# A product that nothing reads behind each quad's factors in the first edge pass of a graph network kernel

## What is computed

```python
# layer 0: attention over edges (8 heads of 12)
score = exp(clip((K[src] * Q[dst] / sqrt(12) * (edge_attr @ We + be)).sum(-1), -5, 5))
h = segment_sum(V[src] * score, dst) / (segment_sum(score, dst) + 1e-6)
# layer 1: mean and maximum of the neighbours, two batch norms
h_mean = segment_sum(x[src], dst) / deg;  h_max = segment_max(relu(x @ W_pool + b_pool)[src], dst)
# layer 2: sum of x[src] * out_deg[src]**-0.5, times in_deg**-0.5, then a 96x96 product
# layer 3: segment_sum((x @ W)[src] * edge_weight, dst)
```

## Time and profile before

| | |
|---|---|
| median of three runs | 5378.2 us |
| profiled execution, whole | 5363.67 us |
| its span, first to last instruction | 5361.9 us |
| TensorE busy with products | 2806.4 us (52%) |
| GpSimd busy | 3210.7 us (60%) |
| VectorE busy | 1951.3 us (36%) |
| ScalarE busy | 1385.4 us (26%) |
| mean granted TensorE clock | 0.641 of full speed |

### The profile page before, as it was taken

How to read it: one execution, slowest core, us unless ns; L and a number is a source line. 1 busy time by engine, 2 the same in 40 slices (tenths; PEclk the granted TensorE clock), 3 DMA queues, 4 the chain that set the end, 5 groups by cost and what they waited for, 6 DMA issues and landing times.

```text
span 5361.9 us, 59693 instructions
## 1 busy us (share of the span) xinstructions
PE 2806.4 (52%) x16706; PEld 2541.5 (47%) x16706; DVE 1951.3 (36%) x4524; ACT 1385.4 (26%) x4351; POOL 3210.7 (60%) x3366
## 2 busy tenths in 40 slices
PE   5655666665567777777775453333334333333334
PEld 5555666665556666666663332323224222222224
DVE  4544444444456555555556111111113221111224
ACT  2111111111243333333334331111112121111113
POOL 4555555555526666666665666666665666666665
PEclk6666666666658888888887555555556555555556
DMA  6655555555532222223321111111111111111111
GB/s 189 172 149 146 146 150 142 151 149 144 151 103 83 82 83 82 82 83 83 83 79 41 34 35 35 35 34 35 35 34 47 35 34 36 35 35 35 35 35 45
DMA packets 337348, 431.81 MB, mean 81 GB/s; under 512 B 99312, under 2 KB 248675, under 8 KB 336941
## 3 DMA queue, kind: packets, MB, share of 16 engines
q0 software_dynamic: 133120, 245.58, 17.5%
q1 hardware_dynamic: 203917, 182.42, 12.1%
HBM read 406.71 MB, written 21.00 MB: 80 GB/s over the span
## 4 chain that ended last, share of the span: by engine, by line
another core or an unknown queue 39%; PE 25%; issue 13%; DVE 10%; ACT 8%; POOL 3%; DMA 1%; ACTq 1%; SPq 0%; DVEq 0%; POOLq 0%
PE bank L642 13%; PE bank L655 3%; DVE same L1561 3%; PE bank L657 3%; PE bank L748 2%; ACT acc L933 2%; POOL rows L550 2%; ACT part_sum L931 1%; DVE prod L1329 1%; DVE score L1331 1%; ACT acc L935 1%; DVE prod L1327 1%; PE bank L741 1%; ACT first_only L1018 1%
## 5 line engine op out<-in xcount | busy, mean ns | idle before, releaser
L642 PE MATMUL bank<-same,rows 128*96 128x128 f32 x4992 | 1025.7, 376 | 1525.0 <-ACT acc L935 573.6
L642 PEld LDWEIGHTS bank<-same,rows 128*96 128x96 f32 x4992 | 880.1, 237 | 1655.8 <-issue 943.7
L550 POOL DMA_INDIRECT rows<-kv_table,src_idx x832 | 790.9, 951 | 709.3 <-DVE msg L1337 460.6
L550 POOL DMA_INDIRECT rows<-pair_table,src_idx x832 | 788.4, 948 | 531.5 <-remote 242.2
L933 ACT COPY acc<-bank 96x511 f32 (+1 forms) x832 | 480.0, 577 | 2365.5 <-remote 1844.8
L550 POOL DMA_INDIRECT rows<-h_table,src_idx x832 | 790.5, 950 | 424.9 <-issue 233.3
L550 POOL DMA_INDIRECT rows<-ci_table,src_idx x832 | 787.0, 946 | 408.7 <-issue 241.7
L1257 DVE TENSOR_TENSOR same<-bank,rank_col 128x512 f32<-128x512 f32 x624 | 421.1, 678 | 990.8 <-remote 621.4
L642 PE MATMUL bank<-same,msg 128*105 128x128 f32 x1664 | 389.5, 409 | 440.5 <-ACT acc L935 430.4
L1561 DVE TENSOR_SCALAR same<-iota_s,rank_col,src_hi 128x128 f32<-128x128 f32 x832 | 235.4, 360 | 896.4 <-remote 728.5
L642 PEld LDWEIGHTS bank<-same,msg 128*105 128x105 f32 x1664 | 337.2, 279 | 462.6 <-DVE same L1257 411.6
(11 more groups left out here) (171 smaller groups left out, 3139.3 us busy)
## 6 DMA issues: line engine op xcount, KB each, us to landing
first_only<-q_table SPq DMA_DIRECT2D x832, 72.0 KB
first_only<-in_attr_cols SPq DMA_DIRECT2D x104, 384.0 KB
first_only<-rank_rows SPq DMA_DIRECT2D x104, 256.0 KB
first_only<-keep_rows SPq DMA_DIRECT2D x104, 192.0 KB
rows<-kv_table,src_idx POOLq DMA_INDIRECT x832
rows<-pair_table,src_idx POOLq DMA_INDIRECT x832
rows<-ci_table,src_idx POOLq DMA_INDIRECT x832
rows<-h_table,src_idx POOLq DMA_INDIRECT x832
```

Source lines behind the costliest of these rows:

```text
L550: pool.indirect_dma_start(rows[:, k, j, 0:width], None, table, bass.IndirectOffsetOnAxis(ap=src_idx[:, t:t + 1], axis=0)).then_inc(rows_in ...
L642: mm = pe.matmul(out[0:nrow, here], left(j), right(j), start=(j == 0), stop=(j == TQ - 1), skip_group_check=True)
```

## The change

One function is added and called at the end of each quad's turn in TensorE's first pass:

```diff
+            def keep_busy(q):
+
+                if q == PREP:
+                    pe.wait_ge(rhs_done, 1)
+                if PREP <= q < ready(0):
+                    pe.matmul(bank[6][:], ident[:], iota_s.rearrange("p (o e) -> p o e", o=1).to_broadcast([P, TQ, P]), start=True, stop=True)
+
             pe.wait_ge(offs_done, 2)
             pe.wait_ge(ready_v, 6)
             factors(0, 0, 0, range(TQ))
@@
                     if static(q) and q == QC - QUERIES + 1:
                         fold_weights()
+                    keep_busy(q)
```

## The result

Seven runs of each kernel: before 5378.2 us median (5372.56 to 5381.17), after 5358.34 us (5350.72 to 5360.62). The ratio is 0.9964, with a 95% interval of 0.9953 to 0.9975: 20 us less, where the forecast had 35 more. The profiled execution of the kernel after took 5357.13 us (span 5355.3), 6.5 us less than that of before, which itself lay 14.5 us under its median.

What follows compares the result with a forecast made beforehand. The prediction took a loop of waits among VectorE, TensorE and ScalarE as the bound. Terms 0 (wait), 0 (second product), +35 (first product) and 0 (clock) took the median from 5378.2 to 5413 us, range 5310 to 5490.

Steps and rivals of the forecast that it cites:

- The loop of waits: First pass: VectorE waits for TensorE's factors, TensorE's aggregate for ScalarE's add; 13.91 us a pair, no engine full.
- The wait at quad 16: The single added wait, for `rhs_done`, was already met at quad 8: 0 us.
- the product behind the second factors: In each pair it runs in a 4.6 us gap before the next first aggregate: 0 us.
- The product behind the first factors: In each pair it delays the second aggregate and second factors by 0.87 to 1.78 us: +35 us in all.
- a floor at 13.16 or 14.07 us: Shortest possible pair, raised by the product from 12.29 us, at full or half clock: 13 or 35 us over 90 pairs.
- the sum 11.40 + 1.78: Short pair: 11.40 us from first aggregate to ScalarE's copy, lengthened by one half-clock product of 1.78 us.
- hidden altogether: Rival: the second aggregate's signal is late anyway and covers the product's delay; 0 us, 5378 us, chance 0.25.
- The clock: First pass: granted clock rises from 0.63 to 0.7 or more, giving back 0 us; rival -65 us, chance 0.20.
- TensorE becomes the bound: Rival: in each pair TensorE's work, signals and two products take 15.04 us against 13.91; +102 us, 5480 us, chance 0.20.

Runs made afterwards that it cites:

- b_again: The kernel before, timed against itself as a control on a later chip: 4467.57 us, ratio 1.0001.
- a_r5: The changed kernel timed a fifth time after the result, beside the kernel before on another chip: 4462.4 us, ratio 1.0002.
- k_two_r2: The changed kernel with the unread product twice behind each quad's factors, against the kernel before: 4460.56 us, ratio 0.9996.
- two_light: The kernel before with every second first-pass gather made a plain load, plus the unread product twice a quad: 4311.21 us, ratio 0.9667 to the kernel before.
- k_six: The unread product six times behind each quad's factors, all gathers kept, against the kernel before: 4933.07 us, ratio 1.106.

## Why the prediction was wrong, point by point

*What bounds the kernel.* The loop of waits was read rightly for the execution at hand, and so was the discrepancy: signals that reach the other engines microseconds after the array's records end. It isn't a property of the kernel. Later, on five chips, the same program took 909 to 918 us less. In the last pass of b_again ScalarE's copy, where it waited, started 0.12 us behind the end of TensorE's last record (median of 179); in the profile of before that median is 1.8 us. A row of the last pass shows the two side by side: what ScalarE waited for, 900 us of before, then 900 us of a_r5.

```profile
ACT acc L933 <- remote: 578.3, 68, 15.6
```

```profile
ACT acc L941 <- PE bank L642: 693.8, 180, 4.4
```

Unmatched, with waits of up to 15.6 us; against matched with TensorE, 180 times for 4.4 us at most. What makes the signals late in the one comparison is open. What the prediction lacked is the bound that takes over where they are prompt: GpSimd needs 9.97 us for a pair's gathers, of which the earlier trace rows already held the larger part (639.89 us busy in 676 gathers, 0.946 each). In the execution it read, with 13.91 us a pair, that bound was not reached.

*The wait at quad 16, and the product behind the second factors: 0.* Right. On the five chips the whole change costs nothing, and with half the gathers one product a quad still costs nothing.

*The product behind the first factors raises the floor of a pair: +35.* This is the step that failed. It said that the distances near 12.0 and 13.4 us would disappear and those at 14.1 and 14.8 stay. Those near 13.4 did go from 14 to 2, but the shortest, near 12.0, became 15 instead of 10, which a floor at 13.16 or 14.07 us forbids. The mechanism's error is in the sum 11.40 + 1.78: it takes the time from the first aggregate to ScalarE's copy for a path that the array's work lengthens. The 15 short pairs after the change show that it isn't: with the second aggregate anywhere from 3.36 to 6.50 us after the first, the copy came at 11.41 to 11.51. So the term of 1.78 measures 0.11 at most in a short pair, and 0 over the pass (mean distance 13.91 both times). Nor was the step needed in the usual pair, where the copy waits for nothing. This is the mechanism of the rival "hidden altogether", whose argument (a delay of 1.78 fits into the 4.7 us between the record and the copy) was in the text and was given less weight than the floor; but its sign, that all groups stay, was not met either, nor its 0 us.

The other chips can't test this term, since GpSimd sets the pair there, but they show a second weakness of the sum. There the shortest distance between two of SyncE's loads up to 1100 us did rise with the products, 6.2, 6.6 and 8.3 us with none, one and two (b_again, a_r5, k_two_r2), and the mean pair stayed at 9.94 to 9.95. A raised shortest pair costs nothing where another engine sets the mean; the forecast had charged each short pair for it.

*The clock: 0.* Right wherever it could be tested. It rose from 0.63 to 0.74, as expected, and from 0.73 to 0.87 on the other chips, and to 0.96 with two products; a pair stayed at 13.91 and at about 9.95 us. On the other chips full clock halves the array's work in a loop whose end GpSimd sets. In the first comparison the signals don't follow the array: in a usual pair VectorE still starts 10.58 us after the aggregate (861.17 to 871.75, with the array at full clock), where it had been 10.60, and the two short pairs above, at half and at full clock, have their copies at 11.51 and 11.46. The Trainium skill's advice in "TensorE: Matmul & The Clock Gate", section "Why this matters for your kernels", to keep TensorE busy without long idle gaps is borne out for the clock. Its price shows in two_light and k_six: past TensorE's room each product costs its full 0.86 us.

*TensorE becomes the bound.* Right as a mechanism, wrong in the place: at full clock the array needs 4.9 + 0.86 n us for a pair with n products. It passes GpSimd's 9.97 us at n = 6 (an estimate from the two equations above; four were measured as free, twelve as not).

*Why 20 us less in the first comparison?* Open. No rule of the prediction gives it: the two profiled executions are 6.5 us apart and none of that is in the first pass, which was 2.7 us longer after the change. It may belong to the condition in which signals are late, through timing that I can't resolve (quads 16 to 196 took 1240.9 us before and 1243.5 after), or to chance beyond the interval. The condition didn't come back in the five later comparisons, so neither the 20 us nor the sequencer's part in the lateness could be tried again.

## What to carry to other kernels

Before a product is added to warm TensorE's clock, count what the slowest issuer needs for the same unit of work: here, on five chips, eight gathers of 1.25 us on GpSimd set the pair, and a clock of 0.96 bought nothing. An idle engine takes added work for nothing until it is full, and from there pays all of it; its room is measured by adding until it costs (here four products of 0.86 us a pair were free). A delay on an engine whose signals arrive late anyway must not be added in full to the path behind it: see first whether the waiting instruction moves when the array's work does.

## What the runs showed of the hardware that was not expected

- One program took 5378 us in the first comparison and 4460 to 4469 us later on five chips (numbers 0, 1, 2, 13 and 15; on which the first comparison ran is not on record). The engines' own instructions are as long in both (a gather 0.948 and 0.946 us, `same` 0.683 us in both); what differs is when waits are released. Why is open.
- In the first comparison ScalarE's copy came 11.41 to 11.51 us after a short pair's first aggregate, whether the array reached the second aggregate after 3.36 or after 6.50 us.
- A gather of 128 rows issued by GpSimd holds it for 0.94 to 0.95 us, and 0.30 us pass before the next: 1.25 us, whether the table's rows are those of the first pass or of the last. A plain load from the same engine holds it for 0.59 us, with no gap before it; a gather that alternates with such loads holds it for 0.98.
- A 128x512 f32 product costs 0.86 us at full clock when TensorE is full, and 1.83 us at half.
